# Gate rows copied by DMA onto four row groups, down codes in two token streams, and the weight quantisation moved into two feed-forward stages

## What is computed

```
x = x + L0_xattn(norm(x), ctx)   # gated products with ctx, by token id
x = x + L0_ffn(norm(x))          # ternary weights, hidden 682
x = x + L1_xattn(norm(x), ctx)   # wkv recurrence
x = x + L1_ffn(norm(x))          # shared expert (352) + 8 routed experts
x = x + L2_xattn(norm(x), ctx)   # softmax attention, 16 heads
x = x + L2_ffn(norm(x))          # ternary weights, hidden 704
x = x + L3_xattn(norm(x), ctx)   # linear attention
x = x + L3_ffn(norm(x))          # weights and inputs rounded to fp8 in blocks of 32
```

```
def _fused_linear(x, W, qa, qb, scale, w):
    out = x @ W.T
    a = jnp.einsum('th,krh->tkr', x, qa)       # 64 "codes" of a token
    b = jnp.einsum('tkr,khr->tkh', a, qb)
    mix = jnp.einsum('tkh,tk->th', b, w)       # codes weighted by w
    return out + scale[None, :] * mix

xe = x + w @ muW.T                             # the "correction"
gate = silu(_fused_linear(xe, gate...))        # 176 inner columns
up = _fused_linear(xe, up...)
out = _fused_linear(gate * up, down...)        # "down codes" inside
y += out * scalar
```

## Time and profile before

| what | value |
|---|---|
| time, median of 3 | 1184.53 us (1170.26 to 1187.07) |
| the profiled execution's own time | 1186.19 us |
| its span, first to last instruction | 1184.5 us |
| mean granted TensorE clock | 0.816 |
| busy PE / DVE / ACT | 1007.4 / 810.0 / 474.9 us |

### The profile page before, as it was taken

One profiled execution on the slowest core, in us unless ns is written; L12 is line 12 of the kernel. 1 busy time (PEld: TensorE's weight loads), 2 busy tenths in 40 slices (PEclk: granted clock), 3 DMA queues, 4 the chain that ended last, 5 costly groups with the idle time before them and its releaser, 6 DMA issues.

```text
span 1184.5 us, 12535 instructions
## 1 busy us (share of the span) xinstructions
PE 1007.4 (85%) x4478; PEld 572.8 (48%) x4478; DVE 810.0 (68%) x1184; ACT 474.9 (40%) x717; POOL 8.9 (1%) x37
## 2 busy tenths in 40 slices
PE   5998854695999999999996799899878887758997
PEld 3445533343555555555554333333356556644565
DVE  3674459745688888885737799999833445656985
ACT  2223447522222221222116799989814333412211
POOL 2000000000000000000000000000000000000000
PEclk8999875796999999999759655555577889968998
DMA  9200012002021111000000488888910000000000
GB/s 286 95 1 1 0 28 33 0 1 57 1 30 30 30 30 27 3 1 0 9 0 1 81 154 151 156 146 151 158 48 1 1 0 1 0 1 1 4 14 18
DMA packets 189721, 51.74 MB, mean 44 GB/s; under 512 B 171407, under 2 KB 188517, under 8 KB 189669
## 3 DMA queue, kind: packets, MB, share of 16 engines
q1 hardware_dynamic: 189668, 51.06, 22.1%
HBM read 20.62 MB, written 1.05 MB: 18 GB/s over the span
## 4 chain that ended last, share of the span: by engine, by line
PE 63%; DVE 24%; ACT 6%; issue 4%; DMA 2%; DVEq 0%; ACTq 0%; SPq 0%
PE ps L725 58%; DVE arena L2135 5%; PE ps L436 2%; PE ps L855 1%; DVE xn_t L1644 1%; ACT xc L1525 1%; DMA arena<-xc 1%; DVE arena L1813 1%; DVE arena L2138 1%; DVE sq L2013 1%; DVE sq L2016 1%; PE ps L1117 1%; DVE xc L1628 1%; ACT sq L1320 1%; PE ps L1284 1%
## 5 line engine op out<-in xcount | busy, mean ns | idle before, releaser
L725 PE MATMUL ps<-arena 128*128 128x16 f16 (+7 forms) x1744 | 314.8, 326 | 33.5 <-DVE arena L2146 7.9
L725 PE MATMUL ps<-arena_split 128*128 128x512 f32 (+6 forms) x832 | 244.8, 447 | 18.7 <-DVE arena_split L1665 11.4
L725 PEld LDWEIGHTS ps<-arena 128*128 128x128 f16 (+4 forms) x1744 | 132.2, 130 | 190.5 <-issue 140.8
L725 PEld LDWEIGHTS ps<-arena_split 128*128 128x128 f32 (+6 forms) x832 | 164.4, 200 | 88.6 <-issue 34.9
L2135 DVE TENSOR_REDUCE arena<-ps 128x1 f32<-128x1024 f32 x128 | 155.6, 1216 | 10.6 <-PE ps L725 10.6
L1525 ACT ACTIVATE xc<-ps,arena 128x1024 int16<-128x1024 f32 x128 | 154.1, 1205 | 19.6 <-DVE arena L2138 11.8
L725 PE MATMUL ps<-sq,arena 128*64 128x512 f32 (+2 forms) x192 | 93.5, 602 | 4.8 <-DVE sq L2016 4.3
L1477 ACT ACTIVATE xc<-ps 128x512 f32<-128x512 f32 x16 | 9.6, 597 | 155.2 <-PE ps L725 155.2
L1355 ACT ACTIVATE act_buf<-ps 128x512 f32<-128x512 f32 (+2 forms) x34 | 20.3, 597 | 99.1 <-PE ps L725 99.1
L436 PE MATMUL ps<-ident,arena 128*128 128x128 f32 (+4 forms) x194 | 36.3, 334 | 19.3 <-DMA arena<-in_x 6.5
L725 PE MATMUL ps<-mean_w,sq 128*128 128x1 f32 x240 | 34.8, 275 | 19.4 <-ACT sq L1320 19.4
(11 more groups left out here) (271 smaller groups left out, 1321.0 us busy)
## 6 DMA issues: line engine op xcount, KB each, us to landing
arena<-in_L_ffn_w SPq DMA_DIRECT2D x4, 640.0 KB, 5.1
arena<-xc SPq DMA_TRANSPOSE x112, 3.3
arena<-in_x SPq DMA_DIRECT2D x1, 1024.0 KB, 5.6
arena<-in_ctx SPq DMA_DIRECT2D x1, 1024.0 KB, 8.1
arena<-in_L_ffn_gate_w SPq DMA_DIRECT2D x1, 1024.0 KB, 8.9
arena<-in_L_ffn_up_w SPq DMA_DIRECT2D x1, 1024.0 KB, 11.3
arena<-in_L_ffn_down_w SPq DMA_DIRECT2D x1, 1024.0 KB, 12.2
arena<-in_L_ffn_gate_W SPq DMA_DIRECT2D x8, 128.0 KB, 2.1
```

Source lines behind the costliest of these rows:

```text
L725: return pe.matmul(o, l, r, start=start, stop=stop)
```

## The change

Four things change in the experts. (1) The masking of the gate rows by DVE is gone; instead SP copies, by 10 small DMAs for each expert, the expert's rows into a tile `gate_rows`: 24 rows at partition 0 and 24 at partition 32 (high, low, high parts of the 8 gate weights), 16 at 64, 2 at 96 (the scalar's two parts). The matching weights `mu_rows` are laid out once by 48 DMAs. With that the correction of a unit is 4 matmuls where it was 10: two for `xe` (partitions 0 and 32), one for the spread weights (64), one for the scalar (96). (2) `down_codes` is four matmuls over 256 tokens each where it was two over 512: the first 256 tokens go to output rows 0 to 63, the others to rows 64 to 127. DVE weights them by two instructions. (3) The correction for unit n + 2 now stands at the end of unit n, and `scalar` and `codes` for n + 1 directly behind `inner`, with the transposes split in two groups around `down_codes`; ACT's and DVE's lists follow. The hardware loops are unrolled. (4) The fp8 rounding of layer 3's weights leaves the experts and goes, as 24 pieces of 256 elements for each partition where it was 12 of 512, behind each chunk of the feed-forward of layer 0 (12 pieces) and of layer 2 (12 pieces). All of the ternary steps of layer 2 move into units 4 to 13.

```diff
+            def rows(tile, r, src, s):
+                sp.dma_start(tile[r:r + src.shape[0]].bitcast(F32), src.bitcast(F32)).then_inc(s, 16)
+
+            sp.wait_ge(mu_split, 1)
+            for f in range(NF):
+                for o in range(KC):
+                    for c_, part in enumerate((0, 0, 1)):
+                        rows(mu_rows[:, f, :], 32 * o + NK * c_,
+                             mu_parts[f * NK:(f + 1) * NK, part, o * P:(o + 1) * P], load["rows"])
+
+            def load_gates(f, part):
+
+                done, tile = load[f"gate{f % 2}"], gate_rows[:, f % 2, :]
+                for r in ((0, 2 * NK, 32, 32 + 2 * NK, 64), (NK, 32 + NK, 64 + NK))[part]:
+                    rows(tile, r, gate_parts[f * NK:(f + 1) * NK, part, :], done)
+                rows(tile, 96 + part, gate_parts[NE + f:NE + f + 1, part, :], done)
+
             sp.wait_ge(x_ready, 2 * LN["l1"] + 4)
             bkv = a["L2_xattn_bkv"]
...
+            sp.wait_ge(rt_gates_sb, 1)
+            load_gates(0, 0)
+            sp.wait_ge(gate_split, 1)
+            load_gates(0, 1)
+            for part in range(2):
+                load_gates(1, part)
+            for f in range(2, NF):
+
+                sp.wait_ge(moe_turn_a, 2 * f - 2)
+                sp.wait_ge(moe_turn_d, 2 * f - 2)
+                load_slot(f, f % 2)
+
+                sp.wait_ge(moe_srm, 2 * f - 2)
+                for part in range(2):
+                    load_gates(f, part)
...
-            def correction(f, s, h):
-                n = f * 2 + h
-                g = [masked[0:GATES, s, j, tok(h)] for j in range(2)]
+            def correction(n):
+
+                f, h = divmod(n, 2)
+                g = gate_rows[:, f % 2, tok(h)]
                 if h == 0:
-                    pe.wait_ge(moe_masked, f + 1)
-
-                    pe.wait_ge(moe_ev_act, f * 2 + 1)
-                if not (isinstance(f, int) and n == 0):
+                    pe.wait_ge(load[f"gate{f % 2}"], 160 * (f // 2 + 1))
+                if n == 0:
+                    pe.wait_ge(load["rows"], 16 * 6 * NF)
+                else:
+
+                    pe.wait_ge(moe_aw, n)
+                pe.wait_ge(moe_ev_act, n + 1)
+                pe.wait_ge(moe_ev_dve, n + 1)
+                mm(ps[:, 0, :], mu_rows[0:3 * NK, f, :], g[0:3 * NK], True, True)
+                mm(ps[:, 1, :], mu_rows[32:32 + 3 * NK, f, :], g[32:32 + 3 * NK], True, True).then_inc(moe_mu, 1)
+                if n:
                     pe.wait_ge(moe_sr, n)
-                mm(ps[:, 7, :], rep_r[0:GATES, :], g[0], True, False)
-                mm(ps[:, 7, :], rep_r[0:GATES, :], g[1], False, True).then_inc(moe_wrm, 1)
-                for o in range(KC):
-
-                    high, low = (mu_parts[0:GATES, j, o * P:(o + 1) * P] for j in range(2))
-                    mm(ps[:, o, :], high, g[0], True, False)
-                    mm(ps[:, o, :], high, g[1], False, False)
-                    last = mm(ps[:, o, :], low, g[0], False, True)
-                last.then_inc(moe_mu, 1)
+                if n == TERN_UNIT + 2:
+                    pe.wait_ge(tern_read, 1)
+                mm(ps[:, 7, :], rep_r[64:64 + 2 * NK, :], g[64:64 + 2 * NK], True, True).then_inc(moe_wrm, 1)
+
+            def scalar(n):
+
+                f, h = divmod(n, 2)
                 pe.wait_ge(moe_wr, n + 1)
-                mm(ps[:, 7, :], sc_rep_r[0:GATES, :], g[0], True, False)
-                mm(ps[:, 7, :], sc_rep_r[0:GATES, :], g[1], False, True).then_inc(moe_srm, 1)
+                mm(ps[:, 7, :], rep_r[96:98, :], gate_rows[96:98, f % 2, tok(h)], True, True).then_inc(moe_srm, 1)
...
                 mm(ps[0:PACK, 4, :], b["qb_restT"], aw, False, True).then_inc(moe_h, 1)
 
             def down_codes(f, s, h):
+
                 n = f * 2 + h
                 pe.wait_ge(moe_hg, n * 2 + 2)
-                mm(ps[0:64, 2, :], slots[s]["dqaT"], moe["h"], True, False)
-                mm(ps[0:64, 2, :], slots[s]["dqa_restT"][64:PACK, :], moe["pack"][64:PACK, :], False, True
-                   ).then_inc(moe_ad, 1)
+                b = slots[s]
+                out = [(ps[64 * j:64 * j + 64, 2, 256 * j:256 * j + 256], slice(256 * j, 256 * j + 256))
+                       for j in range(2)]
+                for o, t in out:
+                    mm(o, b["dqaT"], moe["h"][:, t], True, False)
+                for o, t in out:
+                    last = mm(o, b["dqa_restT"][64:PACK, :], moe["pack"][64:PACK, t], False, True)
+                last.then_inc(moe_ad, 1)
...
             def unit(f, s, h, final):
-                ahead = (f, s, 1) if h == 0 else (f + 1, 1 - s, 0)
+                n = f * 2 + h
                 inner(f, s, h, final)
-                if not final or h == 0:
-                    correction(*ahead)
-                else:
-
-                    pe.wait_ge(moe_sr, 2 * NF)
-                    ternary(2)
+                if n + 1 < 2 * NF:
+                    scalar(n + 1)
+                    codes(n + 1)
+                if not final:
+
+                    pe.wait_ge(moe_sm, 2 * n + 1)
+                    turn_main(f + 1, 1 - s, h == 1)
+                elif h:
                     ln_mean_of("l2x", 0)
                 down_codes(f, s, h)
                 if not final:
-
-                    pe.wait_ge(moe_xe, f * 2 + (h + 2))
-                    (turn_first, turn_second)[h](f + 1, 1 - s)
+                    turn_codes(f + 1, 1 - s, h == 1)
                 result_first(f, s, h)
-                if not final or h == 0:
-                    codes(*ahead)
-                else:
+                if final and h:
                     ln_var_of("l2x", 0)
                 result_second(f, s, h)
-
-            correction(0, 0, 0)
-            codes(0, 0, 0)
-            with pe.Fori(0, NF // 2 - 1) as pair:
-                for s in range(2):
-                    for h in range(TH):
-                        unit(pair * 2 + s, s, h, False)
-            for f in (NF - 2, NF - 1):
+                if n == TERN_UNIT:
+
+                    pe.wait_ge(moe_sr, n + 2)
+                    ternary(2)
+                if n + 2 < 2 * NF:
+                    correction(n + 2)
+
+            correction(0)
+            scalar(0)
+            codes(0)
+            correction(1)
...
+                if n + 1 < 2 * NF:
+                    scalar_rows(n + 1)
                 if not final:
                     (copy_first, copy_second)[h](f + 1, 1 - s)
+                if n + 2 < 2 * NF:
+                    weight_rows(n + 2)
+                    x_high(n + 2)
...
+            def mx_weights(i):
+                v = w_l3_all[:, i, :].rearrange("p (a b) -> p a b", b=MX_BLOCK)
+                step(mx_quant(v, mx_pow, mx_sc[:, 0, :], mx_sc[:, 1, :], 8, step))
...
-            ffn(l0, gate_l0)
+            dve.wait_ge(load["l3"], 16 * 3)
+            ffn(l0, gate_l0, between=mx_weights)
...
-            def mask_gates(f, s):
-                TS(masked[0:GATES, s], gate_parts[0:GATES], group_mask[0:GATES, bass.ds(f, 1)], None, ALU.mult
-                   ).then_inc(moe_masked, 1)
...
-                ahead = (f, s, 1) if h == 0 else (f + 1, 1 - s, 0)
-                if not final or h == 0:
-                    corrected(*ahead)
+                if n + 1 < 2 * NF:
+                    weighted_codes(n + 1)
                 else:
                     ln_xc_of("l2x", 0)
+                if not final:
+                    (copy_first_main, copy_second_main)[h](f + 1, 1 - s)
                 dve.wait_ge(moe_ad, n + 1)
-                TTN(M["pack"][0:64, :], ps[0:64, 2, :], M["wr"][0:64, h, :], ALU.mult).then_inc(moe_awd, 1)
-                if not final or h == 0:
-                    x_low(*ahead)
+                for j in range(2):
+                    t = slice(256 * j, 256 * j + 256)
+                    r = slice(64 * j, 64 * j + 64)
+                    last = TTN(M["pack"][0:64, t], ps[r, 2, t], M["wr"][r, h, t], ALU.mult)
+                last.then_inc(moe_awd, 1)
                 if not final:
-                    (copy_first, copy_second)[h](f + 1, 1 - s)
-                if not final or h == 0:
-                    weighted_codes(*ahead)
-                if not final and h == 0:
-                    mask_gates(f + 1, 1 - s)
-
-                if round_ is not None:
-                    mx_weights(n)
+                    (copy_first_codes, copy_second_codes)[h](f + 1, 1 - s)
                 if final and h:
                     ln_diag_of("l2x", 0)
                 dve.wait_ge(moe_y, n + 1)
                 TTN(x_t[:, :, tok(h)], ps[:, 5:7, :], x_t[:, :, tok(h)], ALU.add).then_inc(moe_x, 1)
-                if h == 1 and round_ is not None:
-                    fold_scales(f + 2, s, round_)
-
+                for i in TERN2.get(n, ()):
+                    tern2(i)
+                if n + 2 < 2 * NF:
+                    corrected(n + 2)
+                    x_low(n + 2)
+                if h == 1 and f + 2 < NF:
```

(23 more changed lines are left out.)

216 lines of the change are left out of this document (96 added, 120 removed).

## The result

| | kernel before | changed kernel |
|---|---|---|
| median, all runs | 1184.9 us (69 runs, 1167.5 to 1192.0) | 1203.3 us (10 runs, 1198.1 to 1206.1) |
| profiled execution, its span | 1186.2, 1184.5 us | 1205.6, 1203.8 us |
| mean granted clock | 0.816 | 0.803 |

Measured beside each other twice, the changed kernel takes 1.0197 times as long (95% interval 1.0127 to 1.0267; 4 runs, median 1202.2 us) and 1.0242 times (1.0198 to 1.0285; 6 runs, 1203.3 us). It is slower by about 2%. One thing must be known to read these ratios: the times of the kernel before fall into two groups, 29 runs at 1167.5 to 1176.6 (median 1172.0) and 40 at 1184.5 to 1192.0 (median 1187.9), with nothing between, and the ratios leave out most of the upper one.

The account below looks back on a forecast made before the run. PE was taken to bound the expert units, a chain from engine to engine the feed-forwards of layers 0 and 2. Profiled 1186.2 - 25 (experts) + 43 (rounding) = 1204, median 1202 us; range for 8 in 10: 1170 to 1230.

Parts of the forecast that it names:

- Loss in layers 0 and 2: Feed-forwards of layers 0 and 2: rounding pieces on DVE delay the chain to PE, together 43 us lost (bounds 11 and 79).
- I give 1 us for each stage: Feed-forwards of layers 0 and 2: allowance for matmuls slowed by the clock falling behind PE's gaps, 1 us a stage.
- Units: The 16 expert units: PE's work falls from 16.8 to 14.2 us a unit, with no idle time left.
- The rival of an array that does not overlap: Expert units: narrow matmuls run one by one or drain between, 15.6 us a unit, time 1219, slower; chance 0.15.
- Ternary steps: Units 4 to 13: 16.4 us of DVE steps on the way to `x_low`, less slack, 12 us late (bounds 5 and 16).
- The slack is under 1 us: At a unit's end: DVE and ACT need 4.8 us before PE needs DVE again, after correction 0.5 and inner 5.2.
- Start of the experts: From the gates' copy to the first `inner`: ten DMAs, scalar rows and a second correction come ahead, 5 us lost.
- Experts in sum: All expert work: 30 us saved in the stage less 5 lost at its start, 25 us gained.

Follow-up runs that it names:

- one-stream run: The changed kernel with the down codes in one stream of 512 tokens again, four float32 passes and not eight half-width ones: 1234.2 us.
- the old places: The changed kernel with layer 2's ternary sums back in the last three units and the comparisons behind the last unit: 1208.6 us.

## Why the prediction was right, and where it was wrong inside

The number held: 1202 forecast, 1203.3 measured, within the range. That it came so close is luck: the terms behind it did not all hold, and their errors cancelled.

- **Loss in layers 0 and 2: right mechanism, one term too small.** The order that was worked out is in the trace: centred input, variance, row sum, last low part, each behind a piece of 3.3 us, the variance at 119.54 where 118.7 plus this run's later start of 0.8 gives 119.5. Idle PE grew by 18.0 and 17.9 us (20 forecast), DVE is busy 61.4 us (65.7 forecast, with the short gaps between a piece's instructions; a piece does take 3.3 us from start to end). The step that failed is "I give 1 us for each stage" for the clock: the same matmuls took 8.4 and 8.3 us longer. In the first half of layer 0 the matmuls from 119.54 to 126.50 at half clock put the row sum at 133.13, where 129.2 + 0.8 = 130.0 was worked out, and the last `down` at 147.40 instead of 143.7. Each stage is 87 us long, not 81 to 82: 52.6 lost against 43. The run without pieces and the one with filled gaps show both parts.
- **Units: right, a little less.** 14.5 to 14.8 us without a ternary step against 14.2 (the terms written down add up to 14.1). The correction's three matmuls take 0.43 (0.5 forecast), down codes 1.17 (1.3); the scalar's one matmul has 0.42 and not 0.3 from its start to the next start, the 24 F32R matmuls 5.8 and not 5.5, the results 3.64 and not 3.4. The rival of an array that does not overlap falls by the common starts and by the one-stream run (0.82 us a unit). Its sum was wrong too: 0.13 more for the correction and 0.9 for the down codes make a unit of 15.2, which fits the 17 us it takes off, and not 15.6.
- **Ternary steps: too dear.** 12 us forecast, 7.3 measured against units without one, 6.0 against the old places. "The slack is under 1 us" was wrong: it took `inner` as 5.2 us, where its own 18 x 0.23 and 2.0 give 6.1, and left the scalar's 0.3 out; with them the slack is 2.1. In the unit ahead of the one shown above, the low part ends at 394.96 and the codes that need it start at 397.4, 2.4 us later. The unit shown has a sum of 1.5 us and takes 14.76, no more than even units without one (14.7 to 14.8).
- **Start of the experts: right.** The first `inner` comes 4.1 us later behind the gates' transposes (5 forecast), the first down codes 5.9, as scalar, codes and four transposes now stand ahead of them. The DMAs are issued every 0.66 us (20 in 13.18), not every 0.46; the correction starts 8.5 us after the gates' copy, not 7.6 (that sum starts at 283.4, 0.6 behind the copy's end, for which there is no row). The 48 DMAs for `mu_rows` took 32.6 us of SP and not 22, but from 257.4 to 290.0, ahead of the gates' copy at 310.7, so nothing waited for them, as forecast.
- **Experts in sum**: 27.3 - 5.9 = 21.4 against 25. Without rounding, and against the lower group of the kernel before, it is 1172.0 - 1151.9 = 20.1. No later unit waits for its gates' DMAs.
- **What was not foreseen**: the projections, -15.5 us between the profiled runs. The prediction said of the ternary steps that they return nothing there, and that is true, but the clock there has two courses. By the groups of times the kernel before takes the long one in 40 of 69 runs, the changed one in none of ten. Within one course the change costs 1203.3 - 1172.0 = 31 us (34.8 by the stretches), not 18. So the forecast of 18 was hit because a loss 10 us too small, a gain 4 us too large and 4 us in other stretches were covered by a change of clock of 15.

## What to carry to other kernels

Work moved into "idle" time of an engine must be placed against the chain, not against the busy share: 24 pieces of 3.3 us cost 51 us in stages in which DVE was idle more than half of the time. Most of the same work (nine or ten of twelve double pieces), split over DVE's gaps in the expert units, costs 5 to 13, and putting the pieces behind the norm steps alone returned 15. Where the move opens gaps on PE, price the matmuls behind them at the lower clock too: here they were a third of the loss. And before a few microseconds are explained, compare stretch by stretch: two groups of times 16 us apart in the unchanged kernel can hide or feign a result.

## What the runs showed of the hardware

- The granted clock stayed at 0.50 for 42 to 43 us while PE was busy without a gap (float32 matmuls of 256 columns). In the changed kernel it was at 1.00 for 22.6 us in a row of the same code, behind two short falls, with the same 1.68 us of idle time ahead.
- Filling gaps with unread matmuls raised the clock in layers 0 and 2 (0.76 to 0.92, 0.86 to 1.00), but not in the 25 us behind the gates, where the filling covered one wait of 8 us and it stayed at 0.50.
- Matmuls on different groups of output columns, with different moving data, overlap as those on different row groups do: pairs of records start within 0.01 us, eight half-width float32 passes take 1.17 us. A narrow F32R group has 0.42 to 0.43 us from its start to the next start, alone or as three, where a full one in a row has 0.24 (18 from 405.30 to 409.61).
